# A fused perceiver layer: second weight store, new order of keys and queries, and a held Pool queue

## The chip, the cores and the metric

The kernel runs on one core of one Trainium2 chip. The metric is the device time of one execution in microseconds, from the profiler of the chip; the kernel before was timed in three runs, and one further execution was profiled.

## The reference

One layer with three residual blocks on x of 2 batches x 128 tokens x 256 features:

```
x = x + cross_attention(layernorm(x), ctx)   # 16 heads, 8 kv heads, 2048 keys per batch, all in use here
x = x + self_attention(layernorm(x))         # 16 heads in 4 groups, causal over 128 tokens
x = x + ffn(layernorm(x))                    # 16 experts, top 2, and one shared expert

# self-attention
q = x @ w_q                 # 256 -> 16*128
k, v = split(x @ w_kv)      # 256 -> 4*128 each
probs = softmax(causal(q k^T / sqrt(128)))
out = (probs v) @ w_dense   # 2048 -> 256

# router of the ffn
scores = sigmoid(x @ gate_w); selected = top2(scores + expert_bias)
weights = scores[selected] / sum(scores[selected])
out = shared(x) + sum over all experts e of comb[:, e] * (silu(g_e) * u_e) @ down_e
```

Everything is float32 at the boundary.

## The kernel before

Accuracy is kept by splitting: most operands are stored as a rounded part (`_hi`, written by ScalarE or VectorE in a float32r type) and the rest (`_lo`, the difference, mostly written by Pool at line 415). A `product` is then three matmuls, lines 550 to 552: lo by hi, hi by lo, hi by hi. Some products (the scores, the attention over values and the transposes of the self-attention) are plain float32 matmuls, which show in the profile as two passes each.

The program is one block with a hand-written instruction order for each engine (TensorE, ScalarE = ACT, VectorE = DVE, Pool = GpSimd, and Sync = SP, which issues nearly all transfers). An engine works strictly in its order, and semaphores with counts connect them. There is no planner: `wait_ge(semaphore, n)` ahead of an instruction holds the engine until the count is reached.

The cross-attention runs over 8 groups of heads (g) and ends near 254 us. Its last moved blocks (`move_blocks`, transfers of transposed probabilities into `pT`) are waited for by Sync before the self-attention's weights are loaded into space that they free.

The self-attention runs over R = 4 groups (r), each with 4 query heads and one key/value head, software pipelined on TensorE. `group2(r, before)` holds the scores of r (`scores2`), the attention over values of r-1 (`attend2`), the queries of r+1 (`queries2`: heads 0 and 1 into the bank QA, heads 2 and 3 into QB), the dense product of r-1 (`dense2`), keys and values of r+1 (`keys_values2`), and the transposes of the probabilities of r (`turn2`). The first group is written out batch by batch ahead of the loop, and `last_group2` holds r = 3, whose dense product accumulates per batch in two banks (`dense_end`). `keep_warm` issues matmuls whose result is never read.

For every r: Sync loads the query weights (`wq2`, 512 KB), the key/value weights and the dense weights (`wd2`). Vector rounds them (`round_q`, `round_kv`, `round_d`; line 1452, the value weights are copied in line 1463), and Pool writes the rest part (`split_q`, `split_k`, `split_d`). There is one raw store and one pair of hi/lo stores for query weights, so `round_q(r+1)` waits until TensorE has finished the queries of r. The last dense weights (r = 3) take over the query weights' store. Softmax of batch b: Vector scales and masks (line 1443) and takes the maximum (1449), Scalar takes the exponential (1171), Vector the reciprocal of the sum (1578), Pool multiplies (`normalise`, 495). Scalar copies the transposed probabilities (1207) and the rounded part of the attention's output (`copy_c`, 1179), Vector its rest (`rest_c`, 1561).

The feed-forward stage starts with the router on Vector: a chain of 20 small instructions (`chained`, each waits for the one before), with `gated` and `rest_h` of the first two hidden blocks placed in between. Expert weights go through a ring of 4: Sync loads, Scalar rounds, Pool writes the rest of gate and up (`split_expert`), Vector the rest of down (line 1689). TensorE needs gate/up m for `gate_up(m)`, and the hidden block's rest part (`rest_h`, line 1639) for `down(m)`.

## Time and profile before

| | before |
|---|---|
| median of 3 runs | 363.52 us (363.18 to 363.71) |
| profiled execution | 363.58 us |
| its span, first to last instruction | 361.8 us |
| granted TensorE clock | 0.991 of full |
| TensorE busy | 335.4 us (93%) |
| TensorE weight loads | 298.9 us (83%) |
| VectorE busy | 278.7 us (77%) |
| ScalarE busy | 230.6 us (64%) |
| Pool busy | 244.7 us (68%) |

An engine's busy time is the sum of its instructions; the timeline of an engine lists them in order, merged where they are alike, and in brackets the idle time ahead of one and the instruction of another engine that ended it. Start times are counted from the first instruction. A name such as `ctxT_hi`, `blocks`, `probs` or `ctx_raw` is that of a large buffer in which the later stages keep their own tiles: in the self-attention `ctxT_hi` and `ctxT_lo` hold weights, `blocks` raw weights, `probs` queries, keys and probabilities; in the feed-forward stage `ctx_hi` and `ctx_lo` hold expert weights and `pT` the hidden block's rest part.

### The profile page before, as it was taken

Reading aid. Unit: us, or ns where it says so; the run is one execution under the profiler, and the core shown is the slowest. Engines: PE = TensorE matmul, PEld = TensorE weight load, DVE = VectorE, ACT = ScalarE, POOL = GpSimd, SP = SyncE. Lnnn points to the kernel's source line nnn. Section 1 sums busy time; section 2 is a strip of 40 time slices with the busy share of each in tenths; the row PEclk is TensorE's granted clock in tenths of the full one; section 3 lists DMA queues with packets and bytes.
Section 4 is the critical chain, followed back from the end, with each engine's and each line's share of the span. In section 5 each row is a group of like instructions: output and inputs, shape, how many; then the busy total and the mean of one; then the engine's idle time right before and its main releaser. Section 6 shows DMA issues by size and latency. Waiting matters only on the chain.

```text
span 361.8 us, 6869 instructions
## 1 busy us (share of the span) xinstructions
PE 335.4 (93%) x2223; PEld 298.9 (83%) x2223; DVE 278.7 (77%) x472; ACT 230.6 (64%) x410; POOL 244.7 (68%) x150
## 2 busy tenths in 40 slices
PE   4796799999999999999999999999889999998996
PEld 1674589988889889889889888899778997688995
DVE  3579788879779779789789788764577765579997
ACT  3458587576867777678668567774235686256762
POOL 4907599598679589678776867959335768524550
PEclk9998799999999999999999999999999999999999
DMA  7603886877885885985975975875216040402630
GB/s 226 204 0 87 207 187 148 205 189 158 200 188 117 207 193 120 209 191 117 204 167 114 205 168 131 199 215 169 85 24 196 13 128 19 144 8 84 187 117 30
DMA packets 33332, 52.07 MB, mean 144 GB/s; under 512 B 5792, under 2 KB 23328, under 8 KB 33312
## 3 DMA queue, kind: packets, MB, share of 16 engines
q1 hardware_dynamic: 33168, 51.56, 56.8%
q10 hardware_dynamic: 144, 0.26, 0.3%
q8 instruction: 10, 0.16, 0.2%
q14 instruction: 10, 0.08, 0.1%
HBM read 20.08 MB, written 0.26 MB: 56 GB/s over the span
## 4 chain that ended last, share of the span: by engine, by line
PE 41%; DVE 21%; issue 16%; SPq 6%; ACT 6%; POOL 5%; DMA 3%; DVEq 1%; ACTq 0%; POOLq 0%
PE pair L550 6%; PE pair L552 6%; PE pair L551 6%; SPq L262 6%; PE bank L550 5%; PE bank L551 5%; PE bank L552 5%; DVE probs L1356 4%; DVE ctx_raw L1367 4%; POOL pT L415 3%; ACT pT_hi L1046 2%; DVE blocks L1367 2%; DVE resid L1386 2%; PE bank L790 2%; POOL ctxT_lo L415 2%
## 5 line engine op out<-in xcount | busy, mean ns | idle before, releaser
L415 POOL TENSOR_TENSOR pT<-pT,pT_hi 128x1024 fp32r<-128x1024 f32 x60 | 142.8, 2406 | 39.3 <-ACT pT_hi L1046 39.2
L1036 ACT ACTIVATE probs<-probs,lowest 128x2048 f32<-128x2048 f32 x32 | 64.4, 2011 | 49.7 <-DVE lowest L1356 49.7
L551 PE MATMUL bank<-pT,ctx_hi 128*128 128x256 f32 x240 | 68.7, 286 | 0.0
L550 PE MATMUL bank<-pT_hi,ctx_lo 128*128 128x256 f32 x240 | 68.1, 284 | 0.0
L552 PE MATMUL bank<-pT_hi,ctx_hi 128*128 128x256 f32 x240 | 68.1, 284 | 0.0
L1046 ACT ACTIVATE pT_hi<-pT 128x1024 fp32r<-128x1024 f32 x60 | 61.5, 1050 | 8.1 <-DMA pT<-blocks 5.0
L550 PE MATMUL pair<-ctxT_hi,qk_lo 128*128 128x512 f32 x128 | 52.9, 413 | 6.3 <-DVE lowest L1356 2.3
L552 PE MATMUL pair<-ctxT_hi,qk_hi 128*128 128x512 f32 x128 | 51.1, 399 | 0.0
L551 PE MATMUL pair<-ctxT_lo,qk_hi 128*128 128x512 f32 x128 | 51.0, 398 | 0.0
L550 PEld LDWEIGHTS bank<-pT_hi,ctx_lo 128*128 128x128 f32 x240 | 45.3, 189 | 1.1
L551 PEld LDWEIGHTS bank<-pT,ctx_hi 128*128 128x128 f32 x240 | 45.1, 188 | 1.1
L415 POOL TENSOR_TENSOR ctx_lo<-ctx_raw,ctx_hi 128x512 fp32r<-128x512 f32 (+1 forms) x19 | 31.2, 1649 | 21.5 <-ACT ctx_hi L1248 19.2
L552 PEld LDWEIGHTS bank<-pT_hi,ctx_hi 128*128 128x128 f32 x240 | 45.7, 190 | 0.0
L1356 DVE CUSTOM_DVE_ANT_0 probs<-pair,mask_bias,lowest 128x1024 f32<-128x1024 f32 x32 | 40.9, 1278 | 3.3 <-PE pair L552 2.8
L1356 DVE CUSTOM_DVE_ANT_0 probs<-pair,mask_bias 128x1024 f32<-128x1024 f32 x32 | 38.5, 1204 | 5.0 <-PE pair L552 5.0
L1367 DVE STREAM_TRANSPOSE blocks<-probs 128x2048 f32<-128x2048 f32 x16 | 36.4, 2307 | 0.0
L550 PEld LDWEIGHTS pair<-ctxT_hi,qk_lo 128*128 128x128 f32 x128 | 24.6, 193 | 11.9 <-DVE lowest L1356 3.6
L1367 DVE STREAM_TRANSPOSE ctx_raw<-probs 128x2048 f32<-128x2048 f32 x14 | 31.9, 2306 | 0.0
L552 PEld LDWEIGHTS pair<-ctxT_hi,qk_hi 128*128 128x128 f32 x128 | 24.6, 192 | 5.6
L415 POOL TENSOR_TENSOR ctxT_lo<-blocks,ctxT_hi 128x1024 fp32r<-128x1024 f32 (+1 forms) x12 | 21.9, 1837 | 8.9 <-DVE ctxT_hi L1452 8.3
L551 PEld LDWEIGHTS pair<-ctxT_lo,qk_hi 128*128 128x128 f32 x128 | 24.8, 193 | 3.2
L1319 DVE TENSOR_TENSOR yT_lo<-bank,yT_hi 128x256 fp32r<-128x256 f32 x16 | 6.8, 425 | 22.9 <-ACT yT_hi L1057 22.9
(234 smaller groups left out, 824.6 us busy)
## 6 DMA issues: line engine op xcount, KB each, us to landing
pT<-blocks SPq DMA_DIRECT2D x128, 128.0 KB, 2.3
pT<-ctx_raw SPq DMA_DIRECT2D x112, 128.0 KB, 2.3
ctx_raw<-ffn_experts_gate_up_dram SPq DMA_DIRECT2D x16, 256.0 KB, 3.1
wq<-in_L_xattn_Wq_dram SPq DMA_DIRECT2D x8, 256.0 KB, 2.7
wo<-in_L_xattn_Wo_dram SPq DMA_DIRECT2D x8, 256.0 KB, 3.0
blocks<-in_L_attn_w_q_dram SPq DMA_DIRECT2D x4, 512.0 KB, 4.0
blocks<-in_L_attn_w_dense_dram SPq DMA_DIRECT2D x4, 512.0 KB, 4.4
ctx_raw<-_L_ffn_experts_down_dram SPq DMA_DIRECT2D x16, 128.0 KB, 2.4
```

The lines of the kernel that those rows point to most:

```text
L262: eng.dma_start(pT[p][LN * q:LN * (q + 1), a].bitcast(F32), blocks[p][LN * a:LN * (a + 1), q]).then_inc(landed[p], 16)
L415: pool.tensor_tensor(dst, src, hi.bitcast(F32), ALU.subtract).then_inc(ready, 1)
L550: pe.matmul(dst, w[1], x[0], start=start, stop=False)
L551: pe.matmul(dst, w[0], x[1], start=False, stop=False)
L552: return pe.matmul(dst, w[0], x[0], start=False, stop=stop)
L790: pe.matmul(PC[b][:], v2[:, b], p2T[:, b], start=True, stop=True).then_inc(c2_psum, 1)
L1036: act.activation(probs[:, j], probs[:, j], ACT.Exp, bias=lowest[:, p, j, 1:2], scale=-1.0, accum_out=den[:, p, j:j + 1]).then_inc(exps, 1)
L1046: act.activation(hi_slot(c), chunk(p, c).bitcast(F32), ACT.Copy).then_inc(pT_hi_ready, 1)
L1319: dve.tensor_tensor(lo[:], src[:, 0:lo.shape[1]], hi[:].bitcast(F32), ALU.subtract).then_inc(ready, 1)
L1356: dve.tensor_tensor_reduce(out=probs[:, j, keys], in0=pair[m % 2][:], in1=mask_bias[:, p, keys], scale=-SCALE, scalar=lowest[:, p, j, 0:1] ...
L1367: dve.transpose(blocks[p][:, :, j].rearrange("p q k t -> p k q t"), probs[:, j].rearrange("p (k q t) -> p k q t", q=QD, t=LN)).then_inc(tu ...
L1386: dve.scalar_tensor_tensor(resid[:, b, :], YO_BANK[:, j * H:(j + 1) * H], rden[:, p, j:j + 1], resid[:, b, :], ALU.mult, ALU.add).then_inc ...
```

## The change

There are six edits.

- Query weights have two stores, used for even and odd r (`wq2_of[r % 2]`), each with its own load semaphore. Sync loads r = 1 before it waits for the last moved blocks, and then r = 0; Scalar rounds the weights of r = 1 once, behind the dense weights of r = 0; Pool splits them right behind `split_d(0)`. Vector no longer rounds r = 1. Later loads, roundings and splits wait for r-2 in place of r-1, and the last dense weights take over the even store one group earlier.
- For batch 1 of r = 0, keys and values are computed between the two halves of the queries. The scores of a batch wait for the second half only ahead of head 2, in every group. Scalar copies the first half of batch 1 ahead of the exponentials of batch 0.
- In the last group the probabilities are transposed into the banks 0 and 2, which are free, in place of the attention's output banks. The order on TensorE is turn, dense, attend for batch 0 and then for batch 1; before, both attends came behind both turns. Scalar copies each attention output behind its own turn copy.
- Vector takes the reciprocal of batch 0 ahead of the rest parts of the group before.
- Pool waits for all 20 steps of the router before it splits the expert weights of the ring's second turn, and `rest_h(1, 1)` moves into the router ahead of its last three steps.
- The loops over r on Sync, TensorE and Vector are written out.

```diff
+        wq2_b = ctx_raw[:, 3072:4096]
+        spare = pT[1].rearrange("p q j k t -> p (q j k t)")
+        wq2_b_hi, wq2_b_lo = spare[:, 0:1024], spare[:, 1024:2048]
+        wq2_of = ((wq2, wq2_hi, wq2_lo), (wq2_b, wq2_b_hi, wq2_b_lo))
+        TURN2_LAST = (bank[0], bank[2])
...
+            def load_q(r):
+                after(sp, wq2_ready, r - 1)
+                sp.dma_start(wq2_of[r % 2][0].rearrange("p (k e) -> p k e", k=HB), sq_v[r]).then_inc(ld_wq2[r % 2], 16)
...
-            load_qkv(0)
+            sp.wait_ge(landed[1], 256 * (G - 1))
+            load_q(1)
+            sp.wait_ge(landed[0], 256 * G)
+            load_q(0)
+            load_kv(0)
             load_d(0)
...
             split_d(0)
+            split_q(1)
             power(1, 1)
-            pool.wait_ge(xn_ready, 2 * B)
-            split_q(1)
             split_k(1)
...
             for b in range(B):
                 power(b, 2)
+            pool.wait_ge(route_step, ROUTER_STEPS)
             with pool.Fori(1, E // RING) as i:
...
             def scores2(r, b):
                 for h in range(HR):
+                    if h == HR // 2:
+                        pe.wait_ge(qb_ready if r or b else first_qb_ready, r + 1)
...
-                attend2(R - 2)
-                keep_warm(QA, 8)
                 for b in range(B):
-                    dense_end(R - 2, b)
-                    turn2(R - 1, b)
-                attend2(R - 1)
-                keep_warm(QA, 1)
+                    attend2(R - 2, b)
+                keep_warm(QB, 8)
+                turn2(R - 1, 0)
+                dense_end(R - 2, 0)
+                attend2(R - 1, 0)
+                turn2(R - 1, 1)
+                dense_end(R - 2, 1)
+                attend2(R - 1, 1)
...
-            queries2(0, of[1])
+            query(0, 0, of[1], qa_psum)
+            query(0, 1, of[1], qa_psum)
             keys_values2(0, of[1], kv2_psum)
+            query(0, 2, of[1], qb_psum)
+            query(0, 3, of[1], qb_psum)
             group2(0, False)
-            with pe.Fori(1, R - 1) as r:
+            for r in range(1, R - 1):
                 group2(r, True)
...
             act.activation(wd2_hi, wd2, ACT.Copy).then_inc(wd2_hi_ready, 1)
+            act.wait_ge(ld_wq2[1], 16)
+            act.activation(wq2_b_hi, wq2_b, ACT.Copy).then_inc(wq2_hi_ready, 1)
...
+            def invert(r, b):
+                dve.wait_ge(s2_exps, HR * (2 * r + b + 1))
+                dve.reciprocal(rd2[:, b], ds2[:, b]).then_inc(s2_rden, 1)
...
                 copy_v(r)
+                invert(r, 0)
                 if before:
                     rest_c(r - 1)
-                for b in range(B):
-                    dve.wait_ge(s2_exps, HR * (2 * r + b + 1))
-                    dve.reciprocal(rd2[:, b], ds2[:, b]).then_inc(s2_rden, 1)
+                invert(r, 1)
...
-            round_q(1)
             round_kv(1)
+            first_qb(1, qb_psum, 1, qb_ready)
...
                 chained(dve.tensor_reduce(total, comb, AX.X, ALU.add))
+                rest_h(1, 1)
                 chained(dve.tensor_scalar(total, total, 1e-20, None, ALU.add))
```

## Rows read from the trace of the kernel before

**Rows 1.** Windows: stretch, length, busy PE, PEld, DVE, ACT, POOL, clock, DMA
```profile
275.00:287.00 12.00, 12.00 (x94) 11.00 (x94) 9.47 (x17) 8.05 (x27) 7.16 (x6) 1.00 0.23 68
327.00:345.00 18.00, 17.60 (x144) 17.13 (x144) 17.29 (x40) 13.28 (x33) 10.08 (x8) 1.00 0.43 132
```
**Rows 2.** Timeline of TensorE, first group: start, us, instruction, idle before it
```profile
266.97 1.13 PE L782 MATMUL bank<-probs 128*128 128x128 f32 x8 [0.46 <-ACT probs L1224]
269.10 0.39 PE L550 MATMUL pair<-xnT_hi,ctxT_lo 128*128 128x256 f32 x1 [1.00 <-POOL ctxT_lo L415]
...
273.64 1.04 PE L821 MATMUL bank<-ident,probs 128*128 128x128 f32 x8
274.79 1.13 PE L782 MATMUL pair<-probs 128*128 128x128 f32 x8
```
**Rows 3.** Timelines of Pool and Vector: the splits, and the second norm's statistics
```profile
254.30 2.37 POOL L415 TENSOR_TENSOR ctxT_lo<-blocks,ctxT_hi 128x1024 fp32r<-128x1024 f32 x1 [0.53 <-DVE xn L1294]
...
266.56 3.23 POOL L415 TENSOR_TENSOR ctxT_lo<-blocks,ctxT_hi 128x1024 fp32r<-128x1024 f32 x2 [5.98 <-DVE ctxT_hi L1452]
...
259.11 0.43 DVE L1284 BATCH_NORM_STATS2 stats<-resid 128x6 f32<-128x256 f32 x1
```
**Rows 4.** Timeline of Vector, first group
```profile
266.76 2.43 DVE L1463 COPY blocks<-blocks 128x256 f32<-128x256 f32 x1
...
274.00 0.68 DVE L1550 COPY probs<-pair 128x512 f32<-128x512 f32 x1
```
**Rows 5.** Timeline of TensorE, last group
```profile
303.89 0.36 PE L550 MATMUL bank<-ctxT_hi,ctxT_lo 128*128 128x256 f32 x1
...
305.60 0.66 PE L821 MATMUL bank<-ident,probs 128*128 128x128 f32 x4
...
307.96 1.98 PE L790 MATMUL bank<-probs 128*128 128x512 f32 x4
...
310.49 0.35 PE L550 MATMUL bank<-ctxT_hi,ctxT_lo 128*128 128x256 f32 x1 [0.33 <-DVE ctxT_lo L1561]
```
**Rows 6.** Timelines of Pool, Scalar and Vector, last group
```profile
298.32 4.70 POOL L415 TENSOR_TENSOR ctxT_lo<-blocks,ctxT_hi 128x1024 fp32r<-128x1024 f32 x2 [0.63 <-DVE ctxT_hi L1452]
304.51 2.04 POOL L495 TENSOR_TENSOR probs<-probs 128x512 f32<-128x512 f32 x2 [1.49 <-DVE probs L1578]
...
309.97 0.60 ACT L1179 ACTIVATE ctxT_hi<-bank 128x512 fp32r<-128x512 f32 x1 [0.35 <-PE bank L790]
...
310.60 0.69 DVE L1561 TENSOR_TENSOR ctxT_lo<-bank,ctxT_hi 128x512 fp32r<-128x512 f32 x1 [0.26 <-ACT ctxT_hi L1179]
...
313.64 0.42 DVE L1604 TENSOR_TENSOR resid<-pair,resid 128x256 f32<-128x256 f32 x1 [0.15 <-PE pair L552]
```
**Rows 7.** Timelines of Pool, Vector and TensorE, router and first experts
```profile
322.59 1.49 POOL L415 TENSOR_TENSOR ctx_lo<-ctx_raw,ctx_hi 128x512 fp32r<-128x512 f32 x1 [6.91 <-ACT ctx_hi L1248]
324.60 1.28 POOL L415 TENSOR_TENSOR ctx_lo<-ctx_raw,ctx_hi 128x512 fp32r<-128x512 f32 x1 [0.52 <-ACT ctx_hi L1248]
...
323.19 0.94 DVE L1659 TENSOR_TENSOR route<-route 128x32 f32<-128x32 f32 x1
324.17 0.19 DVE L1660 TENSOR_TENSOR route<-route 128x32 f32<-128x32 f32 x1
...
324.62 1.29 DVE L1662 TENSOR_SCALAR r<-r 128x2 f32<-128x2 f32 x1
...
328.88 1.14 DVE L1639 TENSOR_TENSOR pT<-ctx_raw,pT_hi 128x256 fp32r<-128x256 f32 x1
...
326.94 0.36 PE L550 MATMUL bank<-ctx_hi,pT 128*128 128x256 f32 x1 [1.48 <-DVE pT L1639]
```
**Rows 8.** The page: instruction queue (packets, MB, share); transfers (KB each, us to landing)
```profile
q8 instruction: 10, 0.16, 0.2%
...
pT<-blocks SPq DMA_DIRECT2D x128, 128.0 KB, 2.3
...
blocks<-in_L_attn_w_q_dram SPq DMA_DIRECT2D x4, 512.0 KB, 4.0
```

More of the change, by code:

```diff
@@ L61, in perceiver_layer @@
     SLOTS = 4
+    ROUTER_STEPS = 20
     LAST = B * G - 1
@@ L234, in perceiver_layer @@
             sem("out_psum"), sem("added"))
-        ld_wq2, ld_wkv2, ld_wd2 = sem("ld_wq2"), sem("ld_wkv2"), sem("ld_wd2")
+        ld_wq2, ld_wkv2, ld_wd2 = [sem(f"ld_wq2_{i}") for i in range(2)], sem("ld_wkv2"), sem("ld_wd2")
         ld_wd2_last, wd2_last_hi_ready = sem("ld_wd2_last"), sem("wd2_last_hi_ready")
@@ L367, in _ @@
                 sp.dma_start(ring_dn[:, m, :], ex_down_w[m - 1]).then_inc(ld_dn[m], 16)
-            load_qkv(1)
-            with sp.Fori(1, R - 1) as r:
-                load_qkv(r + 1)
+            load_kv(1)
+            for r in range(1, R - 1):
+                load_q(r + 1)
+                load_kv(r + 1)
                 load_d(r)
@@ L477, in split_q @@
                 pool.wait_ge(wq2_hi_ready, r + 1)
-                rest(wq2_lo, wq2, wq2_hi, wq2_ready)
+                raw, hi, lo = wq2_of[r % 2]
+                rest(lo, raw, hi, wq2_ready)
             def split_k(r):
@@ L746, in keep_warm, with query @@
                     pe.matmul(where, pT_hi[:, 0, 0:P], pT_hi[:, 0, 0:CH], start=True, stop=True)
-            def query(head, cols, done):
+            def query(r, head, cols, done):
                 dst, h = (QA, QB)[head // 2], head % 2
+                _, hi, lo = wq2_of[r % 2]
                 for k in range(HB):
@@ L761, in queries2 @@
                 for head in range(HR):
-                    query(head, cols, (qa_psum, qb_psum)[head // 2])
+                    query(r, head, cols, (qa_psum, qb_psum)[head // 2])
             def keys_values2(r, cols, done):
@@ L784, in scores2, with attend2 @@
                 mm.then_inc(s2_psum, 1)
-            def attend2(r):
+            def attend2(r, b):
                 pe.wait_ge(v2_ready, r + 1)
-                for b in range(B):
-                    pe.wait_ge(p2T_ready, 2 * r + b + 1)
-                    pe.matmul(PC[b][:], v2[:, b], p2T[:, b], start=True, stop=True).then_inc(c2_psum, 1)
+                pe.wait_ge(p2T_ready, 2 * r + b + 1)
+                pe.matmul(PC[b][:], v2[:, b], p2T[:, b], start=True, stop=True).then_inc(c2_psum, 1)
             def dense2(r):
@@ L832, in group2 @@
                 if before:
-                    attend2(r - 1)
+                    for b in range(B):
+                        attend2(r - 1, b)
                 queries2(r + 1, both)
@@ L1172, in exps2, with copy_c @@
                                    accum_out=ds2[:, b, h:h + 1]).then_inc(s2_exps, 1)
-            def copy_c(r):
-                for b in range(B):
-                    act.wait_ge(c2_psum, 2 * r + b + 1)
-                    act.activation(c2_hi[:, b], PC[b][:], ACT.Copy).then_inc(c2_hi_ready, 1)
+            def copy_c(r, b):
+                after(act, c2_ready, 2 * (r - 1) + b + 1)
+                act.wait_ge(c2_psum, 2 * r + b + 1)
+                act.activation(c2_hi[:, b], PC[b][:], ACT.Copy).then_inc(c2_hi_ready, 1)
             def group2(r, before, behind):
@@ L1184, in group2 @@
                 if before:
-                    copy_c(r - 1)
+                    for b in range(B):
+                        copy_c(r - 1, b)
                 exps2(r, 1)
@@ L1454, in round_q @@
             def round_q(r):
-                after(dve, qb_psum, r)
-                dve.wait_ge(ld_wq2, 16 * (r + 1))
-                round_to(wq2_hi, wq2, wq2_hi_ready)
+                after(dve, qb_psum, r - 1)
+                dve.wait_ge(wq2_hi_ready, r)
+                dve.wait_ge(ld_wq2[r % 2], 16 * (r // 2 + 1))
+                raw, hi, _ = wq2_of[r % 2]
+                round_to(hi, raw, wq2_hi_ready)
             def round_kv(r):
@@ L1573, in group2 @@
                 copy_v(r)
+                invert(r, 0)
                 if before:
                     rest_c(r - 1)
-                for b in range(B):
-                    dve.wait_ge(s2_exps, HR * (2 * r + b + 1))
-                    dve.reciprocal(rd2[:, b], ds2[:, b]).then_inc(s2_rden, 1)
+                invert(r, 1)
                 if split:
@@ L1588, in group2 @@
                     round_d(r)
-            round_q(1)
             round_kv(1)
+            first_qb(1, qb_psum, 1, qb_ready)
             group2(0, False, True, True)
-            with dve.Fori(1, R - 2) as r:
+            for r in range(1, R - 2):
                 group2(r, True, True, True)
@@ L1664, in router @@
                 chained(dve.tensor_tensor(comb, comb, wide(rtotal), ALU.mult))
+                assert flow[0] == ROUTER_STEPS
             def add_expert(m, s):
```

39 lines of the change are left out of this document (17 added, 22 removed).

## The prediction

> **What bounds the kernel now.** I read the table of windows first, then TensorE's timeline through the self-attention for its idle time, then at each idle place the timelines of Vector, Pool and Scalar, and last the page's queues. The windows [rows 1] show TensorE busy all 12.00 us of 275 to 287 and 17.60 of 18.00 us in the feed-forward stretch from 327. In such stretches a faster helper engine buys nothing; a gain must come from a place where TensorE idles. The change touches three such places.
>
> Place 1, the first group (r = 0). TensorE waits 0.46 us for Scalar before the scores of batch 1, and then 1.00 us for Pool: the queries of r = 1 start at 269.10, when Pool has written the rest part of their weights [rows 2]. That split starts at 266.56 [rows 3], because the one store of query weights can be rounded only when r = 0 has read it. A third, small wait: the turns start at 273.64, 16 passes (two rows of 8; 0.11 us each, as the scores' 8 take 0.89) end near 274.5, and the next scores start at 274.79, after Vector's copy of the second query half, 274.00 plus 0.68 [rows 2, 4].
>
> Place 2, the end of the last group. Both attends run back to back at 307.96. The last dense product starts at 310.49 behind 0.33 of waiting, and its second half needs the output of the second attend, which Scalar copies at 309.97 and Vector finishes at 310.60 + 0.69 = 311.29 [rows 5, 6].
>
> Place 3, the router. Two small Vector instructions with operands in SBUF take 0.94 and 1.29 us where their neighbour takes 0.19. Each ends as a Pool instruction ends: 322.59 + 1.49 = 324.08 against 324.13, and 324.60 + 1.28 = 325.88 against 325.91. TensorE then idles 1.48 us until 326.94 for the rest part of the second hidden block, queued behind the router on Vector [rows 7].
>
> The profiled execution is 363.58 us with a span of 361.8, so 1.8 lie around the span; the median of the runs is 363.52, the same within 0.1. I add the steps on the span and subtract from 363.58. Times below are on the clock of the kernel before, less what has been gained by then.
>
> **Part 1: two stores, and keys between the query halves.** The 512 KB of query weights for r = 1 are issued once more ahead of the last wait for moved blocks, instead of after the first split. Each such load lands in 4.0 us [rows 8]; it comes before the load for r = 0, which then lands up to 4.0 us later. On Sync's queue it now stands in front of all loads of the stage. The weights of r = 0 are rounded behind Scalar's last copies of moved blocks, some 8 us after their load is issued in the kernel before, so 4.0 more than its 4.0 just fits: cost taken 0, bound 0 to +1. The later loads of query weights and the last dense weights are issued one group earlier and were hidden before: 0. Scalar gets one more cast of 128x1024, about 1.05 us, behind the dense weights' cast, where it had nothing to do until the last attend was in; cost 0. Pool's split for r = 1 (2.37) goes behind its split at 254.30, which ends at 256.67, so it runs to 259.04. Queued behind it on Pool is the power of batch 1's norm, which needs Vector's statistics started at 259.11 [rows 3]: it fits with 0.07 us before these even begin. If it slips, that path gets up to 0.3 later.
>
> In exchange TensorE finds the weights ready. For batch 1 of r = 0 the order becomes heads 0 and 1, keys and values, heads 2 and 3. The matmuls are the same, so they end at about 266.4 (266.97 less the wait, and 0.1 of drain). The keys' copy on Scalar is then done, so heads 0 and 1 of the scores (0.44) need no wait. Heads 2 and 3 wait for Vector's copy of the second half, issued when the queries' last matmul is out (266.55, plus 0.41, as half of the row of 0.68 and its fixed part): 267.0, or 267.1 if the value weights' copy in front of it is held by Pool's split of the keys. Scores end at 267.55 and the queries of r = 1 start at 267.6 instead of 269.10: **1.5 us**. The probabilities must follow. Before, Vector's masking could not start until the copy at 266.76, which took 2.43 (Pool's split was running), was over at 269.19 [rows 4]; the probabilities were then ready 4.4 later, in time for the turns at 273.64. Now masking starts at 267.8, so they are there at 272.2, and TensorE arrives at 272.1. A cast of Vector's that takes the port ahead of Pool's normalising could add 0.3 there. The wait for the second half before the next scores falls away, as they begin with heads 0 and 1: 0.2 of the 0.29. Together 1.3 to 1.75; I take **1.65**. The groups r = 1 and 2 keep their matmuls and TensorE had no idle time in them [rows 1], so this is carried on whole, and their reordered reciprocals gain nothing.
>
> **Part 2: last group.** Pool's two splits of dense weights end at 298.32 + 4.70 = 303.02. Normalising took from 304.51, 1.02 for each batch [rows 6]; with the reciprocal ahead of the rest parts it can start at 303.05 and batch 0 is ready at 304.1. The warming matmuls end at 303.85, so the turn, now first, waits 0.3. Then, with durations of [rows 5]: turn 0.42 (305.60 to the next dense product), dense 1.5 (1.71 with the change of kind in front), attend 0.66 (a third of 1.98), turn 0.42, dense 1.5, attend 0.66: 304.15 + 0.42 + 1.55 + 0.66 + 0.45 + 1.55 + 0.66 = 309.45. The last dense product of batch 0 can start there, since its context was attended 3.3 earlier and copied meanwhile: 1.0 before 310.49. That of batch 1 may not: it needs its own attend (issued 308.8), about 1.15 to the end of it, Scalar's 0.6, Vector's 0.69: 311.4, against 310.49 + 1.51 = 312.0. The end moves by **0.6**, and Vector's final additions with it (313.64 before [rows 6]). Bounds: 1.0 if the copies overlap better, -0.5 if Pool is as late as before (304.51), for then everything waits behind the turn.
>
> **Part 3: Pool behind the router.** Without the two blockings Vector's route saves 0.94 - 0.19 + 1.29 - 0.19 = 1.85, less 0.34 for the rest part placed inside it (0.42 long, the next starts 0.34 behind its start). That rest part is ready by 324.3 instead of 326.76, so TensorE's 1.48 go. What is behind the wait on Pool: four splits of 1.29 of expert weights. The first starts at 324.9 and ends at 326.2; TensorE, done with the preceding products at 326.0, needs it then: 0.25 idle. The next are due 2.1 apart (18 matmuls of 0.12) and come 1.3 apart. Sync's loads for the ring's next turn wait for these splits, 2.1 later than before for the first, and have over one turn of the ring to land. But they now run one behind the other beside Vector's rest parts, of which one already took 1.14 for 0.42 [rows 7]. Vector is busy 17.29 of 18.00 us there [rows 1], so added blocking reaches TensorE. I count three Vector instructions under the splits, 1.85 of blocking in place of about 1.2. So the stretch gains between 0.05 (rival b) and 2.2 (none of them held: 1.85, and 0.35 for what is held now in the weight ring's later turns). I take **1.4**.
>
> The trace has both orders of Pool and Vector only in part, and here the Trainium skill (SBUF — State Buffer, section "Who interferes with whom") says more: a Vector instruction with two SBUF inputs, or in a two-port mode, and a Pool instruction exclude each other, and the one issued first keeps the port to its end. The rows above agree for two-input instructions. By that rule alone Pool's queued splits would always be there first, which is rival (b) below, at 361.3.
>
> **Sum**: 1.65 + 0.6 + 1.4 = 3.65; 363.58 - 3.65 = 359.93, forecast **359.9**.
>
> **Rivals.** (a) Everything overlaps better: feed-forward 2.2, last group 0.9, first group 1.75, in all 4.85: 358.7. For it: three parts that would each only have to reach their bound. Against it: Vector is nearly full [rows 1]. (b) Pool's splits hold Vector's three instructions to their ends: the first meets a split already 0.85 old and waits 0.45, the others 1.29 each, 3.03 in place of 1.2, so of Vector's 1.85 there is 0.05 left: 363.58 - 1.65 - 0.6 - 0.05 = 361.3. For it: 1.14 for 0.42 at 328.88; against it: Vector's copy was over at 269.19, between two splits of Pool that take until 266.56 + 3.23 = 269.79 together, so a waiting Vector instruction does get in at a boundary [rows 3, 4]. (c) The last group's turn waits for Pool as in the kernel before: part 2 is -0.5 in place of 0.6, 361.0. (d) Slower: the loops over r of TensorE, Vector and Sync are now written out, so each engine fetches new code where it ran a loop. The instruction queue moved ten packets of 16 KB [rows 8]. If a fetch stops TensorE for about as long as a transfer of moved blocks takes to land, 2.3 us, one such stop leaves a gain of 1.35 (362.2), and two make it slower: 4.6 - 3.65, 364.5. It decides from 3.65 us of such stops on. Against it: the straight-line stretches of the kernel before show no such gap on TensorE.
>
> **Chances.** Forecast 0.60 (own range 359.0 to 360.7), (a) 0.13, (b) 0.12, (c) 0.07, (d) 0.08, half of it past the point of decision. The range takes in (a) to (c): 358.5 to 361.6. A measurement of this kernel can tell 0.2%, 0.73 us. Faster, under 362.8: 0.92; within: 0.04; slower: 0.04.
>
> **What would show it.** After: no idle time of TensorE before the queries of r = 1, which start 1.5 earlier; the group of r = 1 starts its scores 1.65 earlier; Pool's split for r = 1 stands before 259.1 and the second norm is not later; the last addition of the stage comes 2.2 earlier; the router's instructions all take about 0.2 and end 1.5 earlier relative to its start; Pool's first expert split starts right behind it. Wrong would be: a new wait of TensorE for Pool's normalising or for the expert weights above 0.5 us, rest parts of Vector over 1 us more than once behind the router, gaps without a releaser in the written-out groups.

## The result, and the profile after

The changed kernel takes 359.27 us (median of 4 runs, 358.98 to 359.83), the kernel before in the same session 363.35 us (4 runs, 362.82 to 363.71). The ratio is 0.9896, with an interval of 0.9878 to 0.9913. The profiled execution is 359.38 us with a span of 357.6, against 363.58 and 361.8: 4.2 us less.

The span is best compared by stretches that begin at an instruction both kernels have. I use four: the transposes of the first norm of the self-attention ("a"), the eight warming matmuls of the last group ("warm"), the router's matmuls ("g"), and the end. TensorE's timeline after the change:

```profile
253.57 0.44 PE L581 MATMUL bank<-ident,xn 128*128 128x128 f32 x2 [0.23 <-DVE xn L1318]
...
298.94 2.39 PE L759 MATMUL pair<-pT_hi 128*128 128x512 f32 x8
...
314.30 1.06 PE L957 MATMUL bank<-gatew,ones 128*128 128x16 f32 x8 [0.47 <-DVE xnT_lo L1323]
```

and before:

```profile
254.27 0.44 PE L568 MATMUL bank<-ident,xn 128*128 128x128 f32 x2 [0.23 <-DVE xn L1294]
...
301.45 2.39 PE L746 MATMUL pair<-pT_hi 128*128 128x512 f32 x8
...
317.56 1.06 PE L938 MATMUL bank<-gatew,ones 128*128 128x16 f32 x8 [0.47 <-DVE xnT_lo L1299]
```

| stretch | before | after | gain | forecast |
|---|---|---|---|---|
| start to a (cross-attention) | 254.27 | 253.57 | 0.70 | 0 |
| a to warm (part 1) | 47.18 | 45.37 | 1.81 | 1.65 |
| warm to g (part 2) | 16.11 | 15.36 | 0.75 | 0.6 |
| g to end (part 3) | 44.24 | 43.30 | 0.94 | 1.4 |

The first 0.70 is not the change's. The earliest that the change does is a load of Sync's, issued at 235.49, and the difference is older: one and the same Vector instruction starts at 225.60 before and at 224.88 after, 28.67 and 28.69 ahead of a (the two rows below). Over the profiles of this study the stretch takes between 252.78 and 254.27 us. Its early part shows a granted clock of 0.89 before and 0.94 after, TensorE doing the same work (windows of both kernels, before and then after; columns as in [rows 1]):

```profile
225.60 0.48 DVE L1373 SCALAR_TENSOR_TENSOR oT_lo<-bank,some_key,oT_hi 128x256 fp32r<-128x256 f32 x1
```

```profile
224.88 0.48 DVE L1397 SCALAR_TENSOR_TENSOR oT_lo<-bank,some_key,oT_hi 128x256 fp32r<-128x256 f32 x1
```

```profile
20.00:50.00 30.00, 24.02 (x112) 18.77 (x111) 25.83 (x38) 20.86 (x29) 16.03 (x6) 0.89 0.49 115
```

```profile
20.00:50.00 30.00, 22.43 (x112) 17.78 (x111) 25.89 (x38) 20.96 (x30) 15.83 (x6) 0.94 0.50 116
```

So 3.50 us belong to the change. In the table below the second stretch repeats within 0.04 us and the third within 0.03 between kernels that have the same parts of the change there. The last is less exact: its end is taken from spans that are given to 0.1 us, and a late load disturbs it in three profiles. The medians of the kernel before over the four sessions lie between 362.97 and 363.66 and its single runs between 361.79 and 364.81, so I argue from stretches.

**First group.** TensorE after, which answers to [rows 2]. The queries of r = 1 stand at a + 13.17 in place of a + 14.83 and wait for nothing. The scores of batch 1 ahead of them start without a wait, but their eight passes take 1.39 in place of 1.13: heads 2 and 3 wait for Vector's copy of the second query half, which ends at 266.22 (Vector's row below). The forecast had this wait.

```profile
265.60 1.39 PE L798 MATMUL bank<-probs 128*128 128x128 f32 x8
266.74 0.36 PE L563 MATMUL pair<-xnT_hi,pT 128*128 128x256 f32 x1
...
271.27 1.30 PE L837 MATMUL bank<-ident,probs 128*128 128x128 f32 x8
272.40 1.06 PE L798 MATMUL pair<-probs 128*128 128x128 f32 x8
```

Pool after, to [rows 3]: the split for r = 1 runs at 255.92, and the norm's power finds Pool idle for 1.01 us, so it is not late:

```profile
255.92 2.40 POOL L426 TENSOR_TENSOR pT<-ctx_raw,pT 128x1024 fp32r<-128x1024 f32 x1
259.32 0.56 POOL L422 TENSOR_TENSOR rstd<-var_eps,minus_half 128x1 f32<-128x1 f32 x1 [1.01 <-DVE var_eps L1312]
...
270.42 1.44 POOL L507 TENSOR_TENSOR probs<-probs 128x512 f32<-128x512 f32 x1 [0.44 <-DVE probs L1592]
```

The last of these rows is the new limit: Pool's normalising of batch 1 takes 1.44 where that of batch 0 took 1.04; Vector's cast began 0.16 ahead of it, and with the cast moved behind it (experiments 5 and 9) it takes 1.04. Vector:

```profile
265.80 0.42 DVE L1460 COPY probs<-pair 128x256 f32<-128x256 f32 x1 [0.80 <-PE pair L565]
...
270.26 0.69 DVE L1476 CAST ctxT_hi<-blocks 128x1024 fp32r<-128x1024 f32 x1
...
271.93 2.45 DVE L1489 COPY blocks<-blocks 128x256 f32<-128x256 f32 x1
```

**Last group.** TensorE, Pool and Vector after, to [rows 5, 6]. The turn starts 0.09 us behind the last warming matmul's end (298.94 + 2.39 = 301.33). The first matmul of the last dense product is listed at 306.54 with 0.68 us, while the attend ahead of it still runs, so I compare the second ones: 307.06, 8.12 behind warm, against 310.69, 9.24 behind it. The first half of the product is thus 1.12 earlier. Its second half waits 0.3 and starts at 308.67, 9.73 behind warm against 312.00 - 301.45 = 10.55. TensorE after:

```profile
301.42 0.66 PE L837 MATMUL pair<-ident,probs 128*128 128x128 f32 x4
...
306.54 0.68 PE L563 MATMUL bank<-ctxT_hi,ctxT_lo 128*128 128x256 f32 x1
307.06 0.28 PE L564 MATMUL bank<-ctxT_lo,ctxT_hi 128*128 128x256 f32 x1
...
308.67 0.36 PE L563 MATMUL pair<-ctxT_hi,ctxT_lo 128*128 128x256 f32 x1
```

and before:

```profile
309.37 0.79 PE L746 MATMUL pair<-pT_hi 128*128 128x512 f32 x1
...
310.69 0.28 PE L551 MATMUL bank<-ctxT_lo,ctxT_hi 128*128 128x256 f32 x1
...
312.00 0.28 PE L550 MATMUL pair<-ctxT_hi,ctxT_lo 128*128 128x256 f32 x1
```

The first of these rows is a warming matmul between the attends and the last dense product; the new order leaves it out. It had ended at 310.16, before the rest part that the product waited for (Vector, 309.65 + 0.69 = 310.34), so it was not the limit there. Pool and Vector after:

```profile
295.54 4.69 POOL L426 TENSOR_TENSOR ctxT_lo<-blocks,ctxT_hi 128x1024 fp32r<-128x1024 f32 x2 [0.73 <-DVE ctxT_hi L1476]
300.32 1.04 POOL L507 TENSOR_TENSOR probs<-probs 128x512 f32<-128x512 f32 x1
```

```profile
310.38 0.42 DVE L1633 TENSOR_TENSOR resid<-pair,resid 128x256 f32<-128x256 f32 x1 [0.53 <-PE pair L565]
```

**Router.** Vector, Pool and TensorE after, to [rows 7]. The two small instructions take 0.18 and 0.16 in place of 0.94 and 1.29. Pool's four splits start right behind the router and run as one block, and the rest part of down 4 takes 1.52 under them:

```profile
319.94 0.18 DVE L1688 TENSOR_TENSOR route<-route 128x32 f32<-128x32 f32 x1
...
320.94 0.16 DVE L1692 TENSOR_SCALAR r<-r 128x2 f32<-128x2 f32 x1
...
322.47 0.88 DVE L1668 TENSOR_TENSOR pT<-ctx_raw,pT_hi 128x256 fp32r<-128x256 f32 x1 [0.48 <-ACT pT_hi L1289]
...
324.21 0.58 DVE L1668 TENSOR_TENSOR pT<-ctx_raw,pT_hi 128x256 fp32r<-128x256 f32 x1
324.71 1.52 DVE L1720 TENSOR_TENSOR ctx_lo<-ctx_raw,ctx_hi 128x256 fp32r<-128x256 f32 x1
```

```profile
321.78 5.59 POOL L426 TENSOR_TENSOR ctx_lo<-ctx_raw,ctx_hi 128x512 fp32r<-128x512 f32 x4 [9.36 <-DVE route L1694]
```

```profile
323.20 0.38 PE L563 MATMUL pair<-xnT_hi,ctx_lo 128*128 128x256 f32 x1 [0.29 <-POOL ctx_lo L426]
...
327.40 0.39 PE L563 MATMUL bank<-ctx_hi,pT 128*128 128x256 f32 x1 [0.39 <-DVE resid L1701]
```

TensorE's one wait of 1.48 has become 0.29 and 0.39. What is left of the gain shows in the starts of TensorE's products, counted from g:

| product | before | after | gain |
|---|---|---|---|
| `down(1)` | 9.38 | 7.74 | 1.64 |
| `gate_up(4)`, which needs Pool's first split | 10.17 | 8.90 | 1.27 |
| `down(2)` | 11.58 | 10.42 | 1.16 |
| `down(3)` | 13.97 | 13.10 | 0.87 |
| `down(4)` | 16.20 | 15.33 | 0.87 |

The waits of 0.29 and 0.39 are counted from the modelled end of the matmul before, so they are not what the starts lose: 0.37 at `gate_up(4)`, 0.11 on the way to `down(2)` and 0.29 at `down(3)`, which had a smaller delay of its own before. Behind the router Vector is the full engine, 17.71 of 18.00 us, to the second of [rows 1]:

```profile
324.00:342.00 18.00, 17.30 (x143) 16.84 (x142) 17.71 (x40) 12.45 (x32) 11.25 (x9) 1.00 0.57 167
```

### The profile page after: what moved, and what is told of

Read it like the earlier page. It is cut to its first block, busy times and chain, and to the rows that moved or that the text cites. A ratio compares the mean times of both kernels' runs of the same rounds, so it can differ in the third digit from the quotient of the medians.

```text
span 357.6 us, 6832 instructions
## 1 busy us (share of the span) xinstructions
PE 332.4 (93%) x2222; PEld 297.5 (83%) x2222; DVE 275.1 (77%) x471; ACT 231.2 (65%) x411; POOL 245.4 (69%) x150
## 4 chain that ended last, share of the span: by engine, by line
PE 43%; DVE 23%; issue 15%; ACT 7%; POOL 5%; SPq 2%; DMA 2%; DVEq 1%; ACTq 0%; POOLq 0%
PE pair L563 7%; PE pair L565 6%; PE pair L564 6%; PE bank L563 6%; PE bank L564 5%; PE bank L565 5%; DVE ctx_raw L1391 5%; DVE probs L1380 5%; POOL pT L426 3%; ACT pT_hi L1065 3%; SPq L268 2%; ACT probs L1055 2%; DVE resid L1410 2%; DVE resid L1701 2%; PE bank L805 1%
## 5 line engine op out<-in xcount | busy, mean ns | idle before, releaser
L563 PE MATMUL pair<-ctxT_hi,qk_lo 128*128 128x512 f32 x128 | 52.1, 407 | 6.3 <-DVE lowest L1380 2.4
L426 POOL TENSOR_TENSOR ctxT_lo<-blocks,ctxT_hi 128x1024 fp32r<-128x1024 f32 (+1 forms) x10 | 17.1, 1723 | 7.1 <-DVE ctxT_hi L1476 6.6
```

The costliest lines, as they stand in the source:

```text
L426: pool.tensor_tensor(dst, src, hi.bitcast(F32), ALU.subtract).then_inc(ready, 1)
L563: pe.matmul(dst, w[1], x[0], start=start, stop=False)
```

## The experiments

All stretches in us, from one profile of each kernel; g to end is the span less g. Ratios are to the kernel before, run beside it. "One run" marks a single timed execution, which has no interval.

| kernel | median | ratio (interval) | a to warm | warm to g | g to end |
|---|---|---|---|---|---|
| before | 363.35 | 1 | 47.18 | 16.11 | 44.24 |
| after | 359.27 | 0.9896 (0.9878, 0.9913) | 45.37 | 15.36 | 43.30 |
| 1 without part 3 | 360.43 | 0.9912 (0.9890, 0.9933) | 45.37 | 15.34 | 43.65 |
| 2 part 3 alone | 361.68 | 0.9949 (0.9931, 0.9967) | 47.20 | 16.11 | 42.88 |
| 3 without part 1 | 361.26 | 0.9938 (0.9919, 0.9957) | 47.17 | 15.35 | 42.84 |
| 4 part 2 alone | 362.37 | 0.9966 (0.9950, 0.9982) | 47.16 | 15.35 | 44.19 |
| 5 paced | 358.80 | 0.9887 (0.9861, 0.9913) | 45.58 | 15.34 | 42.51 |
| 6 loops alone | 362.55 | 0.9990 (0.9967, 1.0012) | 47.78 | 16.11 | 43.74 |
| 7 keys behind | 360.54 | 0.9925 (0.9896, 0.9955) | 45.78 | 15.34 | 42.80 |
| 8 hold alone | 359.05 | one run | 45.36 | 15.33 | 42.51 |
| 9 combined | 358.86 | 0.9876 (0.9858, 0.9895) | 45.05 | 15.35 | 42.40 |
| 10 combined, one pace | 358.19 | 0.9863 (0.9842, 0.9884) | 45.05 | 15.34 | 42.47 |
| 11 reciprocals behind | 360.18 | one run | 45.37 | 17.01 | 42.84 |

**1 to 4: each part by itself.** Without part 3, from the changed kernel:

```diff
-            pool.wait_ge(route_step, ROUTER_STEPS)
...
-                rest_h(1, 1)
...
             router()
+            rest_h(1, 1)
```

> The changed kernel without its third part (Pool does not wait for the router, the rest part of the second hidden block is again behind the router). My theory: the three parts act in three stretches one after the other and add up; part 3 is worth the 0.92 us by which the stretch from the router's logits to the last expert product is shorter in the changed kernel. So 359.3 + 0.9 = 360.2, with both small Vector instructions of the router at 0.9 us or more again. Rival (a slack theory: the feed-forward stretch is bound by Vector or the weight ring, and the router's gain is given back): 359.3 to 359.6.

Part 3 alone is the reverse of this edit on the kernel before.

> The kernel before with part 3 alone. My theory: 0.9 us faster than before (the same 0.92 as in the changed kernel), TensorE's idle 1.5 us ahead of the second expert's down product gone, and two new waits of 0.3 to 0.4 for Pool's split and for Vector behind it. Rival of full gain: 1.5 us faster, if the two new waits are special to the changed kernel's phases. Rival of no gain: within 0.2 us of before.

Without part 1 is the kernel before with parts 2 and 3 and the reciprocal's place:

```diff
+            pool.wait_ge(route_step, ROUTER_STEPS)
...
-                attend2(R - 2)
-                keep_warm(QA, 8)
                 for b in range(B):
-                    dense_end(R - 2, b)
-                    turn2(R - 1, b)
-                attend2(R - 1)
...
+                turn2(R - 1, 0)
+                dense_end(R - 2, 0)
+                attend2(R - 1, 0)
...
+                invert(r, 0)
```

> Parts 2 and 3 on the kernel before, without part 1 (one store of query weights, keys behind all queries of batch 1, scores waiting for both query halves, loops kept as loops). My theory: part 1 is worth 1.7 to 1.8 us, so 359.3 + 1.75 = 361.1, and TensorE waits again about 1.0 us for Pool at the queries of r = 1. If the written-out loops cost or gain something of their own, this differs from the sum of the other parts: a cost of 2 us or more per stop for code would show as 359.3 or less here.

Part 2 alone is the same without the two edits at the router.

> The kernel before with part 2 alone: turns into free banks, turn, dense, attend for each batch, Scalar's copy behind each turn, and the reciprocal of batch 0 ahead of the rest parts. My theory: 0.75 us faster than before, the last addition of the stage 0.75 earlier after the last scores. Rival: the turn now waits for Pool's normalising, 1.7 us late, and it is 0 to 0.5 slower.

Measured: the three parts act in three separate stretches. Part 1 takes a to warm from 47.2 to 45.37 with part 3 or without it. Part 2 takes warm to g from 16.11 to 15.35 in both kernels that have it without part 1. The router, g to the start of its last step, takes 8.57 in kernels 1 and 4 and 7.04 in 2 and 3. The wait that part 3 removes is in kernel 1 as it was before:

```profile
323.51 0.35 PE L562 MATMUL bank<-ctx_hi,pT 128*128 128x256 f32 x1 [1.47 <-DVE pT L1667]
```

The last stretch has one disturbance of its own. Without part 3 it takes 44.2 (before, 4) or 43.7 (1, 6), and with it 43.30 (after) or 42.8 to 42.9 (2, 3, 7, 11), other edits apart. Where it is longer Scalar waits for a late load of gate/up weights (before, after and 4, and no other kernel of the table). Kernel before against kernel 6, which has the same code there: the cast stands at g + 17.13 against 16.68, Pool's split behind it at 17.84 against 17.38, Vector's rest part takes 1.31 against 1.02, and TensorE's `down(6)` starts at 20.92 against 20.47. Scalar's rows of before and of after:

```profile
334.69 0.63 ACT L1248 ACTIVATE ctx_hi<-ctx_raw 128x512 fp32r<-128x512 f32 x1 [0.34 <-DMA ctx_raw<-ffn_experts_gate_up_dram]
```

```profile
334.93 0.63 ACT L1272 ACTIVATE ctx_hi<-ctx_raw 128x512 fp32r<-128x512 f32 x1 [0.47 <-DMA ctx_raw<-ffn_experts_gate_up_dram]
```

Like with like, part 3 is worth 0.94 with the late load (44.24 to 43.30) and 0.8 to 0.9 without it (43.65 and 43.74 to 42.84). Counted to the start of Vector's last addition, where no rounding of the span comes in, it is 0.91 (41.47 to 40.56) and some 0.86 (from 40.96 and 40.97 to between 40.09 and 40.14).

**5: paced.** In the changed kernel Pool's splits 3 and 4 of the four wait until Vector has written the rest part of the down weights two before them; and Vector's cast of the first group goes behind its copy of queries.

```diff
+            for s in range(RING):
+                if s >= 2:
+                    pool.wait_ge(dn_ready, RING + s - 1)
+                split_expert(1, s)
-            with pool.Fori(1, E // RING) as i:
+            with pool.Fori(2, E // RING) as i:
...
-                if split:
+                if split and before:
                     round_q(r + 2)
...
                     copy_qb(r + 1)
+                if split and not before:
+                    round_q(r + 2)
```

> The changed kernel with two edits. One: of the four expert splits behind the router, Pool's third waits for Vector's rest part of the down weights of expert 4, and the fourth for that of expert 5, so that they no longer stand in front of it on the shared port. Two: in the first group Vector's cast of the query weights of r = 2 stands behind its copy of the second query half, so that it no longer holds Pool's normalising of batch 1. My theory: the 1.52 us rest part falls to 0.4, and TensorE's wait of 0.39 at the down product of expert 3 goes: 0.3 to 0.4 in the stretch from the router's logits to the end; and 0.25 in the stretch from the norm's transposition to the scores of r = 1 (18.83 us in the changed kernel). In all 0.6 us faster than the changed kernel. Rival: Vector's total is the bound and the wait comes back later: only the 0.25. Rival: Pool's third split, now late, makes TensorE wait at expert 6: 0 to 0.3 slower in that stretch.

Measured: the rest part of down 4 takes 0.41 and the expert stretch 0.79 less, 0.46 of which is the late load that is absent here; 0.33 remain. In the first group the scores of r = 1 start at a + 18.57 in place of 18.83, but the gain is lost again and a to warm is 0.21 longer. The value weights' copy takes 2.46 under Pool's split, as it did in the changed kernel (2.45), but with the cast in front it starts 0.19 later (a + 18.55 against 18.36), and TensorE, which is 0.26 earlier, then waits for a rest part of Vector's. Vector:

```profile
272.02 2.46 DVE L1493 COPY blocks<-blocks 128x256 f32<-128x256 f32 x1
...
324.62 0.41 DVE L1726 TENSOR_TENSOR ctx_lo<-ctx_raw,ctx_hi 128x256 fp32r<-128x256 f32 x1
```

TensorE:

```profile
278.84 0.36 PE L567 MATMUL bank<-ctxT_hi,ctxT_lo 128*128 128x256 f32 x1 [0.30 <-DVE ctxT_lo L1591]
```

**6: the written-out loops alone**, in the kernel before. It tests rival (d).

```diff
-            with pe.Fori(1, R - 1) as r:
+            for r in range(1, R - 1):
...
-            with dve.Fori(1, R - 2) as r:
+            for r in range(1, R - 2):
...
-            with sp.Fori(1, R - 1) as r:
+            for r in range(1, R - 1):
```

> The kernel before with the loops over r of TensorE, Vector and Sync written out, nothing else. My theory: 0 within 0.1 us in the stretch from the norm's transposition to the router's logits (63.29 us in the kernel before), at most one packet more of instructions. Rival (the fourth of the prediction): one or more stops of TensorE for code of 2 us each. Rival: waits against constants are cheaper than against registers, and the stretch is 0.1 to 0.3 shorter.

Measured: 0.9990 with an interval of 0.9967 to 1.0012, no difference that can be told. But a to warm is 0.6 longer in its one profile, where within 0.1 was expected (the last stretch has no late load and is 0.5 shorter), and TensorE shows one gap in it, put down to "issue": it stands before the scores of r = 1, and ends 0.10 behind Vector's copy (274.32 + 0.68), as before (0.11, [rows 2, 4]). So it is no stop for code but a wait for Vector, which waits 1.60 for the query weights of r = 2 (0.95 before). TensorE, Vector and Sync:

```profile
275.10 1.13 PE L782 MATMUL pair<-probs 128*128 128x128 f32 x8 [0.73 <-issue]
```

```profile
273.71 0.69 DVE L1452 CAST ctxT_hi<-blocks 128x1024 fp32r<-128x1024 f32 x1 [1.60 <-DMA blocks<-in_L_attn_w_q_dram]
...
274.32 0.68 DVE L1550 COPY probs<-pair 128x512 f32<-128x512 f32 x1
```

```profile
268.76 0.37 SPq L342 DMA_DIRECT2D blocks<-in_L_attn_w_q_dram  x1
```

Vector and Sync before:

```profile
273.36 0.72 DVE L1452 CAST ctxT_hi<-blocks 128x1024 fp32r<-128x1024 f32 x1 [0.95 <-DMA blocks<-in_L_attn_w_q_dram]
```

```profile
269.21 0.38 SPq L342 DMA_DIRECT2D blocks<-in_L_attn_w_q_dram  x1
```

Sync issued the load no later (a + 14.79 against a + 14.94); it was in 4.95 after its issue in place of 4.15. This may well be the edit's doing. In the four kernels that keep Sync's loop (before, 2, 3, 4) the load is in 4.06 to 4.21 after its issue, and its dense weights are issued at a + 16.85; written out, they are issued at a + 16.52, closer behind. One profile does not prove it, and the cause stays open. So the stops for code of rival (d) are not there, but that writing the loops out is free in the first group is not shown. In the changed kernel the same cast is at 270.26 and waits for nothing, since the load runs a group ahead: so part 1 also takes this wait away, which I had not seen in the profile.

**7: keys behind both query halves**, with the second store. It takes part 1 apart.

```diff
-            query(0, 0, of[1], qa_psum)
-            query(0, 1, of[1], qa_psum)
+            queries2(0, of[1])
             keys_values2(0, of[1], kv2_psum)
-            query(0, 2, of[1], qb_psum)
-            query(0, 3, of[1], qb_psum)
...
-            round_kv(1)
             first_qb(1, qb_psum, 1, qb_ready)
+            round_kv(1)
```

> The changed kernel with keys and values of batch 1 (r = 0) behind all four query heads again; the second store, the early split and the split wait of the scores are kept. My theory: most of part 1 comes from the second store. Without the new order the scores of batch 1 wait about 0.46 for Scalar's copy of the keys as before, so the queries of r = 1 start 0.2 to 0.5 later after the norm's transposition than the 13.17 us of the changed kernel. Rival: the order is what brings it (TensorE would otherwise wait for Pool's split of the keys or for the probabilities), 1 us or more later.

Measured: the queries of r = 1 start at a + 13.58 and the scores of r = 1 at a + 19.24; with the new order at 13.17 and 18.83; before, 14.83 and 20.52. So the order is 0.41, and the second store with the rest of part 1 is 1.28. The wait of 0.46 for Scalar's copy of the keys [rows 2] is back, and it is what the order removes:

```profile
265.48 1.13 PE L798 MATMUL bank<-probs 128*128 128x128 f32 x8 [0.46 <-ACT probs L1246]
```

**8: the hold without the moved rest part.** `rest_h(1, 1)` back behind the router, Pool's wait kept.

```diff
-                rest_h(1, 1)
                 chained(dve.tensor_scalar(total, total, 1e-20, None, ALU.add))
...
             router()
+            rest_h(1, 1)
```

> The changed kernel with Pool's wait for the router kept and the rest part of the second hidden block behind the router again. My theory: the router ends 0.34 earlier (1.85 instead of 1.54 less than in the kernel before), but the rest part comes at about 7.1 us after the logits' start, 0.3 to 0.4 before Pool's first split would hold it, or is held by it to 8.0: TensorE waits 0 to 0.4 at the second down product, at 7.74 in the changed kernel, and the end of the stretch is the same within 0.3, since the next product waits for Pool's split in either case. Rival: it must stand inside the router, and the stretch is 0.5 or more longer.

Measured: the router ends 0.33 earlier (g + 6.71), `down(1)` starts at the same g + 7.74, and g to end is 42.51 against 42.84 with the rest part inside (both without a late load; to the start of Vector's last addition, which needs no rounded span, 39.84 against 40.10 in kernel 7). Moving it in is a loss of about 0.3: nobody needed it sooner, and it delayed the router, and with it Pool's first split. Of the wait of 0.29 for this split 0.03 are left.

**9 and 10: the version that should be faster still.** The diffs are against the changed kernel and against kernel 9, and show the main lines. Experiment 8's order, the pace of 5 (all of it in 9, one wait in 10), the cast behind the copy, and the value weights of r = 2 and 3 copied by Scalar, in the same place.

```diff
+                if s >= 2:
+                    pool.wait_ge(dn_ready, RING + s - 1)
...
-                dve.tensor_copy(wv2, wv2_raw).then_inc(wv2_ready, 1)
+                if r == 1:
+                    dve.tensor_copy(wv2, wv2_raw).then_inc(wv2_ready, 1)
...
+                if r < R - 2:
+                    act.wait_ge(wv2_ready, r + 2)
+                    act.wait_ge(ld_wkv2, 32 * (r + 3))
+                    act.activation(wv2, wv2_raw, ACT.Copy).then_inc(wv2_ready, 1)
```

> The changed kernel with four edits: the rest part of the second hidden block back behind the router, Pool's third and fourth expert split behind Vector's rest parts of experts 4 and 5, Vector's cast for r = 2 behind its copy of the second query half (first group), and Scalar instead of Vector copies the value weights of r = 2 and 3. My theory: each removes a collision on Vector that a trace showed. Stretch from the norm's transposition to the last group's warming matmuls: 45.0 to 45.1 instead of 45.37 (the 0.26 won at the scores of r = 1 now stays, since Vector no longer waits 2.4 us for Pool there). Stretch from the logits to the end: 42.2 instead of 42.84 to 43.30. In all 0.9 us faster than the changed kernel. Rival: Scalar's copy delays the exponentials of the next group or the second group waits for Pool elsewhere: first stretch 45.4 or more.

```diff
-                if s >= 2:
+                if s == 2:
```

> As the run before, but only Pool's third split waits (for expert 4), the fourth follows it at once. My theory: the wait of 0.5 us at the down product of expert 5 in the paced kernel came from the later fourth split, so here it is shorter and the last stretch 0 to 0.3 us shorter than in the run before. Rival: it comes from Vector's own total, and both kernels have the same end within 0.1.

Measured: a to warm 45.05, 0.32 less than the changed kernel, so the cast's place now keeps what it gives. g to end 42.40 and 42.47, where 42.2 was expected for 9: the pace brings only 0.1 on top of 8, and with one wait or two the end is the same within 0.1, as the rival of 10 had it. No instruction of Vector's is held over 0.2 us under the first splits now, but one is further on (1.54 for 0.41, last row), and TensorE waits 0.37 behind it: the pace moves the holding more than it removes it. Vector of kernel 9, both places:

```profile
270.98 1.36 DVE L1484 CAST ctxT_hi<-blocks 128x1024 fp32r<-128x1024 f32 x2
...
324.27 0.41 DVE L1730 TENSOR_TENSOR ctx_lo<-ctx_raw,ctx_hi 128x256 fp32r<-128x256 f32 x1
...
328.15 1.54 DVE L1679 TENSOR_TENSOR pT<-ctx_raw,pT_hi 128x256 fp32r<-128x256 f32 x1
```

Against the changed kernel without its late load (42.84) the two gain 0.32 + 0.4 = 0.7 to 0.8 us. The medians, 358.86 and 358.19 against 359.27, agree in sign; the intervals of the ratios overlap (0.9876 and 0.9863 against 0.9896), so whole times do not show this gain, only the stretches do.

**11: reciprocals behind the rest parts**, as before, in the changed kernel. It tests rival (c).

```diff
-                invert(r, 0)
                 if before:
                     rest_c(r - 1)
+                invert(r, 0)
                 invert(r, 1)
```

> The changed kernel with both reciprocals behind the rest parts, as in the kernel before. My theory: Pool's normalising of batch 0 in the last group then starts about 1.5 us later after the warming matmuls' start than the 1.48 of the changed kernel, TensorE's first turn waits for it, and the stretch from the warming matmuls to the last addition grows from 11.44 by 1.0 to 1.4 us. Rival: the copies of the context are the limit there, and it grows by less than 0.3.

Measured: warm to g 17.01 in place of 15.36. The turn, now first on TensorE, waits for Pool, which waits for the reciprocal. TensorE and Pool:

```profile
302.60 0.66 PE L837 MATMUL pair<-ident,probs 128*128 128x128 f32 x4 [1.76 <-POOL probs L507]
```

```profile
301.50 2.04 POOL L507 TENSOR_TENSOR probs<-probs 128x512 f32<-128x512 f32 x2 [1.48 <-DVE probs L1592]
```

## Why the prediction was right

359.9 was forecast, 359.27 measured. By its own terms the profile should have shown 363.58 - 3.65 = 359.93; it showed 359.38. Of this 0.55, 0.70 come from the cross-attention, which the change does not move, and -0.15 from the terms: 1.81 + 0.75 + 0.94 = 3.50 in place of 3.65. The three terms erred by 0.16, 0.15 and -0.46 of gain and nearly cancelled: that part of the match is luck.

**Part 1, forecast 1.65, measured 1.81.** The 1.5 at the queries of r = 1 measured 1.66 (14.83 to 13.17): they were forecast at 267.6 and stood at 254.27 + 13.17 = 267.44 on that clock. The loads, Scalar's cast and Pool's split cost nothing, as forecast. The 0.2 for Vector's copy did not come: 20.52 to 18.83 is 1.69, 0.03 more than the queries gained. The step named the reason as a possible 0.3: Vector's cast ahead of Pool's normalising (270.26 and 270.42). Kernels 5 and 9, with the cast later, start these scores 0.26 earlier. A further 0.12 came between r = 1 and r = 2 (11.87 before, 11.75 after), where "carried on whole" allowed for nothing; it is not the loops, since kernel 6 has 11.86 there. Half of it is the scores themselves: before, behind a wait, the first eight passes took 0.96 to the start of the next eight (274.79 to 275.75), and after they take 0.90 (272.40 to 273.30). The other half I did not isolate. Its absence from the bound, 1.75, is why 1.81 lies outside it.

**Part 2, forecast 0.6, measured 0.75.** Its chain held: the first half of the last dense product moved by 1.12 (forecast 1.0), and the second half, which needs its own attend copied and split, by less, 0.75 to 0.8. The turn's wait, forecast 0.3, was 0.09; these 0.21 cover the difference of 0.15. That the reciprocal is what allows this was only argued in the prediction; experiment 11 shows it: without it part 2 would be 0.75 - 1.65 = -0.90, below the bound of -0.5. Rival (c) is thus a real mechanism, and the change's fourth edit is what removes it. The statement that the reordered reciprocals gain nothing in the earlier groups holds: kernel 11 has the same 45.37 from a to warm.

**Part 3, forecast 1.4, measured 0.94 (0.8 to 0.9 without a late load on either side).** This is the mis-sized term. Its pieces were close: the router 1.85 - 0.34 = 1.51 shorter, measured 8.58 to 7.04 = 1.54; the wait for Pool's first split 0.25, measured 0.29; Vector's three held instructions 1.85, measured (0.88 - 0.42) + (0.58 - 0.41) + (1.52 - 0.41) = 1.74; and the held instructions of the kernel before about 1.2, measured 0.72 + 0.08 + 0.35 = 1.15 (1.14, 0.50 and 0.77 for 0.42). What failed is the last step, from these pieces to 1.4: they give 1.51 - (1.85 - 1.2) = 0.86, and TensorE's starts show 0.87 from `down(3)` on. The 1.4 was taken between the bounds 0.05 and 2.2 and set neither the 0.34 nor all of the 0.65 of added blocking against the gain. And the 0.34 of the rest part placed inside the router was put down as its price without a question what it buys: experiment 8 shows that it buys nothing and costs about 0.3.

**Rivals.** (a) is not refuted by the time: 359.27 lies 0.57 above its 358.7 and 0.63 below the forecast. The stretches refute it as a whole, 3.50 against 4.85; part 1 alone reached its value (1.81 against 1.75), the last group has 0.75 against 0.9 and the experts 0.94 against 2.2. (b) named the right place but too large a price: 1.74 held instead of 3.03. Its wait of 0.45 for the first of the three came as 0.46 and that of 1.29 for the third as 1.11, but the second waited only 0.17; a Vector instruction already waiting gets in between two queued splits, as [rows 3, 4] had suggested. The Trainium skill (SBUF — State Buffer, section "Who interferes with whom") has the mechanism right here, Vector's two-input instructions being held to the end of one Pool instruction (0.88 and 1.52 above); what made rival (b) too dear was the assumption that the second meets a split at its start. (d), stops of TensorE for code, is refuted by experiment 6: the instruction queue moves 11 packets in place of the 10 of [rows 8], and TensorE's one gap there is a wait for a copy. The 0.6 us that this kernel's first group is longer stays open.

One reading of the prediction was wrong without effect: the turns of the first group are 8 passes, not 16 (the rows at 273.64 and 271.27 list eight); each transpose shows as one pass, unlike the scores, and the description of the kernel before is wrong on this too. The end that it worked out, 274.5, is that of 8.

## What to carry to other kernels

Read a small change stretch by stretch, from instructions that both kernels have: here that is exact to 0.04 us where no late load comes in, while whole times move by a microsecond and more with the part of the kernel that nobody touched. Where Pool is moved out of the way of a chain on Vector, its work comes later in one block and holds Vector again; if Vector is nearly full there, subtract every price that you have written down before you name the gain, and move nothing into the chain that nobody waits for. An engine whose work is brought forward needs its whole chain of suppliers brought forward: the new order of the last group is worth 0.75 us with the early reciprocal and -0.90 without it.

## What was unexpected of the hardware

- Pool holds Vector also for a plain copy or cast with one input in SBUF: the value weights' copy took 2.45 under a split of Pool's and 0.28 alone, and a `TENSOR_SCALAR` on 2 columns took 1.29 [rows 7] and 0.16 alone. Vector's instructions with an operand from TensorE's banks kept their time beside the same splits (the hidden block's product, 256 columns, 0.41 to 0.43).
- It goes the other way as well: Pool's normalising takes 1.44 in place of 1.04 when a cast of Vector's began just ahead of it, and 1.04 again where the cast was moved behind it (experiments 5 and 9).
- Loads move by as much as the terms of this case. A late load of gate/up weights costs the last stretch some 0.46 us (43.30 against 42.84) in three of thirteen profiles (before, after and 4), which have no part of the change in common. The 512 KB of query weights for r = 2 were in 4.06 to 4.21 us after their issue in four profiles and 4.95 in the one with Sync's loop written out, where the next loads are issued sooner; whether that is the reason is not shown.
